# Graph attention on one core: the spread of the queries as two one-pass products of 256 columns

## The reference

```python
q = (x @ Wq + bq).reshape(n, 8, 16); k, v = the same with Wk, Wv
scores = sum(q[targets] * k[sources], -1) * 0.25 + (edge_attr @ We + be)
e = exp(scores - segment_max(scores, targets)[targets])
probs = e / (segment_sum(e, targets) + 1e-10)[targets]
agg = segment_sum(probs[:, :, None] * v[sources], targets)
out = layernorm(x + agg @ Wo + bo)
```

## Time and profile before

| | |
|---|---|
| median of 3 runs | 2608.14 us (2605.48 to 2614.73) |
| the profiled execution | 2609.25 us, span 2607.4 us |
| PE matmul | 1395.8 us busy, 54%; 9699 records, and as many loads of weights |
| DVE | 1341.0 us busy, 51% |
| POOL | 1521.0 us busy, 58% |
| ACT | 420.9 us busy, 16% |
| mean granted clock of TensorE | 0.647 of full speed |
| DMA | 290.29 MB, mean 111 GB/s |

### The profile page before, as it was taken

One profiled execution on the slowest core, in us unless ns is written; L12 is line 12 of the kernel. 1 busy time (PEld: TensorE's weight loads), 2 busy tenths in 40 slices (PEclk: granted clock), 3 DMA queues, 4 the chain that ended last, 5 costly groups with the idle time before them and its releaser, 6 DMA issues.

```text
span 2607.4 us, 30805 instructions
## 1 busy us (share of the span) xinstructions
PE 1395.8 (54%) x9699; PEld 933.4 (36%) x9699; DVE 1341.0 (51%) x3136; ACT 420.9 (16%) x1427; POOL 1521.0 (58%) x1578
## 2 busy tenths in 40 slices
PE   4145555455645464555555555546464545555557
PEld 3033333333433343333334333334343333333334
DVE  4045455554555554545555545555454545555556
ACT  0011111111111111111111111111111111111112
POOL 6735656566566566565556565656566665656540
PEclk7555666666667666666666666666566666566666
DMA  7423333333333333333333333333333333333320
GB/s 271 140 82 97 117 103 103 118 102 124 100 118 106 120 103 121 101 109 113 101 119 105 118 108 117 104 116 106 120 104 123 100 124 95 108 117 106 119 88 7
DMA packets 115466, 290.29 MB, mean 111 GB/s; under 512 B 45765, under 2 KB 53712, under 8 KB 108264
## 3 DMA queue, kind: packets, MB, share of 16 engines
q0 software_dynamic: 75072, 205.10, 26.3%
q1 hardware_dynamic: 37484, 76.52, 8.7%
q10 hardware_dynamic: 2748, 6.69, 0.7%
HBM read 276.52 MB, written 11.67 MB: 111 GB/s over the span
## 4 chain that ended last, share of the span: by engine, by line
another core or an unknown queue 37%; PE 34%; DVE 18%; issue 8%; ACT 2%; DMA 1%; SPq 0%; DVEq 0%; ACTq 0%
PE q_banks L1133 12%; PE ps_a L1170 7%; DVE prod L780 4%; DVE score L791 3%; PE ps_e L1145 2%; PE ps_t L1110 2%; PE ps_s L1191 2%; DVE wv L801 1%; PE ps_t L1116 1%; DVE run_fwd L843 1%; PE ps_a L1212 1%; PE ps_s L1197 1%; PE ps_a L1222 1%; DVE cand L837 1%
## 5 line engine op out<-in xcount | busy, mean ns | idle before, releaser
L507 POOL DMA_INDIRECT kv_buf<-kv_table,src_i x1564 | 1499.1, 959 | 1013.8 <-DVE wv L801 569.0
L1133 PE MATMUL q_banks<-q_blk,hots 64*128 64x128 f32 x3128 | 416.4, 405 | 537.3 <-issue 263.0
L1133 PEld LDWEIGHTS q_banks<-q_blk,hots 64*128 64x128 f32 x3128 | 319.4, 277 | 655.1 <-issue 635.0
L567 ACT ACTIVATE hots<-ps_t 128x512 f32<-128x512 f32 x377 | 225.1, 597 | 1972.9 <-PE ps_t L1116 960.8
L780 DVE TENSOR_TENSOR prod<-q_banks,kv_buf 128x512 f32<-128x512 f32 (+1 forms) x392 | 269.0, 686 | 410.8 <-remote 265.5
L801 DVE TENSOR_TENSOR wv<-kv_buf,ps_w 128x512 f32<-128x512 f32 (+1 forms) x392 | 265.6, 678 | 362.8 <-remote 334.8
L1170 PE MATMUL ps_a<-wv,hots 128*64 128x136 f32 x3128 | 376.5, 379 | 5.6 <-ACT wv L608 4.8
L1212 PE MATMUL ps_a<-sums_sb,carry_from 128*1 128x136 f32 x112 | 34.3, 409 | 542.2 <-DVE sums_sb L911 542.2
L791 DVE TENSOR_REDUCE score<-prod 128x32 f32<-128x512 f32 (+1 forms) x392 | 267.1, 681 | 7.9 <-issue 0.2
L1170 PEld LDWEIGHTS ps_a<-wv,hots 128*64 128x64 f32 x3128 | 239.9, 183 | 68.3 <-issue 51.2
L1212 PEld LDWEIGHTS ps_a<-sums_sb,carry_from 128*1 128x1 f32 x112 | 4.8, 81 | 564.1 <-DVE sums_sb L911 564.1
(11 more groups left out here) (141 smaller groups left out, 1337.5 us busy)
## 6 DMA issues: line engine op xcount, KB each, us to landing
edge_f<-in_edge_blk SPq DMA_DIRECT2D x55, 1024.0 KB
kv_buf<-kv_table,src_i POOLq DMA_INDIRECT x1564
kv_table<-kv_buf ACTq DMA_DIRECT2D x12, 512.0 KB, 4.4
xt_blk<-in_x_t SPq DMA_DIRECT2D x114, 32.0 KB
out<-y_out SPq DMA_DIRECT2D x114, 32.0 KB
kv_buf<-in_x_perm SPq DMA_DIRECT2D x5, 512.0 KB, 7.8
codes<-code_table SPq DMA_DIRECT2D x108, 10.5 KB
code_table<-kv_buf SPq DMA_DIRECT2D x1, 1344.0 KB
```

The lines of the kernel that those rows point to most:

```text
L507: pool.indirect_dma_start(kv_buf[:, b % NBUF, t, :], None, kv_table, bass.IndirectOffsetOnAxis(ap=src_i[:, column:column + 1], axis=0)).th ...
L567: one = act.activation(hots[:, v % 2, :, :].rearrange("p k n -> p (k n)"), ps_t[:, :], ACT.Relu, bias=1.0)
L1133: one = pe.matmul(ps_q[j][:, k * D:(k + 1) * D], hots[own, (v - 1) % 2, 0, k * P:(k + 1) * P], q_blk[own, b % QBUF, :], start=True, stop=True)
```

## The change

`spread_q` no longer makes four matmuls of 64 rows. For each pair of tiles it makes two matmuls of 128 rows and 256 columns, which accumulate in PSUM. The moving operand is `q_part`, in the rounded 32-bit format (float32r): for each half of the window its own 128 columns, with zeros in the other half's rows, once with the rounded queries (part 0) and once with what the rounding left (part 1). So a pair's 128 rows give both tiles at once. `hots` has that format too, and the sums by node read it as float32 through a bitcast.

- Removed: `q_blk`, and per step four matmuls of 64x128 by 64x128 float32.
- Added on PE: per step four matmuls of 128x128 by 128x256 float32r.
- ACT `copy_q`: three copies (64x128, 64x128, 128x128) in place of one, and a wait for `s_qlow` of the block before.
- DVE: `low_q`, two subtractions of 64x128, at the end of slot 6 of every block (three of them ahead of the loop), and one memset of 128x1536 in the setup.
- PSUM: a step's queries stand in one bank, steps alternate between two, and the spread of step q waits for the multiply of step q-2, no longer q-1.

```diff
-        hots = sb("hots", [P, 2, 2, QUAD * W])
+        hots = sb("hots", [P, 2, 2, QUAD * W], F32R)
-        q_blk = sb("q_blk", [P, QBUF, D])
+        q_full = sb("q_full", [P, D])
+        q_part = sb("q_part", [P, QBUF, 2, 2 * D], F32R)
-        q_banks = ps("q_banks", [P, 2, 512])
-        ps_q = [q_banks[:, i, :] for i in range(2)]
+        ps_q = [ps(f"ps_q{i}", [P, 512]) for i in range(2)]
             def copy_q(b):
                 act.wait_ge(s_newq, b + 1)
+                if b >= 1:
+                    act.wait_ge(s_qlow, b)
                 if b >= QBUF:
                     act.wait_ge(s_byedge, FIRST[b - QBUF + 1])
-                act.copy(q_blk[:, b % QBUF, :], new_q).then_inc(s_qcopied, 1)
+                act.copy(q_part[0:W, b % QBUF, 0, 0:D], new_q[0:W, :])
+                act.copy(q_part[W:P, b % QBUF, 0, D:2 * D], new_q[W:P, :])
+                act.copy(q_full[:, :], new_q).then_inc(s_qcopied, 1)
+            dve.memset(q_part[:, :, :, :].rearrange("p b k d -> p (b k d)").bitcast(F32), 0.0)
+            def low_q(b):
+                dve.wait_ge(s_qcopied, b + 1)
+                dve.tensor_tensor(q_part[0:W, b % QBUF, 1, 0:D], q_full[0:W, :], q_part[0:W, b % QBUF, 0, 0:D], ALU.subtract)
+                dve.tensor_tensor(q_part[W:P, b % QBUF, 1, D:2 * D], q_full[W:P, :], q_part[W:P, b % QBUF, 0, D:2 * D],
+                                  ALU.subtract).then_inc(s_qlow, 1)
             def multiply(q):
-                dve.tensor_tensor(prod[:, q % 2, 0:n * D].rearrange("p (k j d) -> p j k d", j=2, d=D),
-                                  q_banks[:, :, 0:n // 2 * D].rearrange("p j (k d) -> p j k d", d=D),
-                                  kv_buf[:, b % NBUF, t0:t1, 0:D].rearrange("p (k j) d -> p j k d", j=2),
-                                  ALU.mult).then_inc(s_product, 1)
+                dve.tensor_tensor(prod[:, q % 2, 0:n * D].rearrange("p (t d) -> p t d", d=D),
+                                  ps_q[q % 2][:, 0:n * D].rearrange("p (t d) -> p t d", d=D),
+                                  kv_buf[:, b % NBUF, t0:t1, 0:D], ALU.mult).then_inc(s_product, 1)
+                    if chain(v, 6) is not None and chain(v, 6) + QBUF < NB:
+                        low_q(chain(v, 6) + QBUF)
             def spread_q(v):
-                pe.wait_ge(s_qcopied, b + 1)
+                pe.wait_ge(s_qlow, b + 1)
                 pe.wait_ge(s_copied, HOTS_TO[v - 1])
-                if q >= 1:
-                    pe.wait_ge(s_product, q)
-                for u in range(t1 - t0):
-                    j, k = u % 2, u // 2
-                    own = slice(j * W, (j + 1) * W)
-                    one = pe.matmul(ps_q[j][:, k * D:(k + 1) * D], hots[own, (v - 1) % 2, 0, k * P:(k + 1) * P],
-                                    q_blk[own, b % QBUF, :], start=True, stop=True)
+                if q >= 2:
+                    pe.wait_ge(s_product, q - 1)
+                for k in range((t1 - t0) // 2):
+                    for part in range(2):
+                        one = pe.matmul(ps_q[q % 2][:, k * 2 * D:(k + 1) * 2 * D], hots[:, (v - 1) % 2, 0, k * P:(k + 1) * P],
+                                        q_part[:, b % QBUF, part, :], start=(part == 0), stop=(part == 1))
             def sum_step(v):
-                    one = pe.matmul(sums(b)[own, :], hots[:, (v - 1) % 2, 1, u * W:(u + 1) * W], wv[:, q % 2, u, :],
+                    one = pe.matmul(sums(b)[own, :], hots.bitcast(F32)[:, (v - 1) % 2, 1, u * W:(u + 1) * W], wv[:, q % 2, u, :],
```

More of the change, by code:

```diff
@@ L283, in graph_attention @@
         s_weighted, s_beside, s_summed = sem("s_weighted"), sem("s_beside"), sem("s_summed")
-        s_newq, s_qcopied = sem("s_newq"), sem("s_qcopied")
+        s_newq, s_qcopied, s_qlow = sem("s_newq"), sem("s_qcopied"), sem("s_qlow")
         s_changes, s_runends = sem("s_changes"), sem("s_runends")
@@ L941, in _ @@
             with dve.If(general == 0):
+                for b in range(min(QBUF, NB)):
+                    low_q(b)
                 for v in SLOTS:
```

## The result

| | before | after |
|---|---|---|
| median of 20 runs of each, on one chip | 2610.67 us (2601.36 to 2624.11) | 2622.47 us (2609.46 to 2629.64) |
| ratio | | 1.0045, interval 1.0029 to 1.0060 |
| the profiled execution | 2609.25 us, span 2607.4 | 2614.39 us, span 2612.6 |
| matmul records of PE | 9699 | 8135 |
| mean granted clock of TensorE | 0.647 | 0.654 |

The account below looks back on a forecast made before the run. It took POOL's gathers, held up by DVE's weighting because PE's results come late while gathers are in flight, as the bound. Gains 8 + 50 + 5 less 3 of costs make 60 us: 2548 us, range 2450 to 2660.

Parts of the forecast that it names:

- What bounds the kernel: Steady block of 44.1 us: POOL waits for DVE's weighting because PE's results come late while gathers are in flight.
- PE, fast stretches: Spread on the chain of slots 1 and 2: match begins after 1.0 us instead of 1.16; 8 us less.
- PE, late stretches: Spread while gathers fly: eight fewer matmuls and loads bring later sums forward, 0.9 us a block; 50 us less.
- Second bank: Slot 6: the spread need not wait for the multiply; nothing alone, its effect counted in the 50 us.
- The start: First steps of the kernel: spread of step 1 about 10 us instead of 20.5; 5 us less, ends 0 and 20.
- Costs: Slot 6: ACT's extra copies and DVE's subtractions, mostly covered; 3 us more in all.
- A: Drains stay, since lateness ignores PE's instruction count or sums still miss the drain; 10 us less, 2598; chance 0.25.
- B: DVE and ACT of slot 6 are the bound, each block pays 0.9 us; 50 us more, 2658; chance 0.15.
- C: Spread's rounded products are not one-pass, 3.4 us per spread; 250 us more, 2860; chance 0.05.
- D: PE stops being late, the waits of 3.0 and 3.8 us go; some 370 us less, 2240; chance 0.07.

Follow-up runs that it names:

- turns_and_crossing: Changed kernel with PE's turn_ends first in slot 1 and DVE's crossing_maxima in slot 2 behind the weighting; 2534.24 us, ratio 0.9677 to the kernel before.
- no_low_part: Changed kernel with one ACT copy of the queries and no DVE subtraction from the fourth block on; 2055.09 us, ratio 0.9998 to the kernel before.
- crossing_later_old: Kernel before with crossing_maxima, DVE's two scans, moved one slot later to slot 2 behind the weighting; 2054.15 us, ratio 0.9989.

## Why the prediction was wrong

**What bounds the kernel.** Right for late chips: POOL starves, and results come late while gathers are in flight. Halving the gathers took 795 us away. But I held it for a property of the kernel; on chips in time the bound is POOL's 35.1 us a block. The changed kernel itself did not run there, but with `crossing_maxima` moved in both, the two forms take 2054.42 and 2054.15 us: the change is worth nothing.

**PE, fast stretches (-8).** The match begins 1.02 us after the first matmul of the spread (1342.93 to 1343.95 in the changed kernel), 1.0 forecast and 1.16 before. But the multiply starts 1.26 us after it. The 1.26 of the earlier trace rows was read where DVE was busy until 0.09 us before; where it stood idle for the result, it was 1.27:

```profile
1313.80 1.23 PE L1133 MATMUL q_banks<-q_blk,hots 64*128 64x128 f32 x8
1315.07 0.69 DVE L780 TENSOR_TENSOR prod<-q_banks,kv_buf 128x512 f32<-128x512 f32 x1 [0.38 <-PE q_banks L1133]
```

What DVE waits for became no shorter, so the 8 us could not come.

**PE, late stretches (-50).** This step failed. Its first half came true: the spread of step 1 fell from 20.51 to 9.28 us, 10 forecast. What failed is the step from there to the block: "I take 0.9 us a block, about one wait of 3.4 in four blocks". I counted drain waits by their number and gave each one price. Their number stayed at two a block, and their price depends on what DVE has queued between the late result and the weighting that POOL waits for. With the new spread DVE gets one slot further before each drain, from slots 5 and 1 to 6 and 2, and so the second drain falls ahead of the scans: 3.6 + 6.3 = 9.9 us in place of 3.0 + 3.8 + 2.0 = 8.8. The prediction said "the next step is late in its place" and never asked which instructions that next place has ahead of its weighting. `turns_and_crossing` is the evidence that this order is what hides the gain: with the scans out of that place the same spread gives 3.2% on one late chip, and the same moves without it, on another, nothing. How much of this is the scans' 3.35 us themselves is not shown, since the two moves also spread the waits over other steps.

One term of that sum was also mis-read. The 2.9 us of lateness at 1324.93 are 4.13 less 1.26, but 1.26 belongs to a granted clock of 0.5; at 1323.15 the clock was 1.00 and the same spread was back after 0.76 us:

```profile
1323.15 0.71 PE L1133 MATMUL q_banks<-q_blk,hots 64*128 64x128 f32 x8
1323.91 0.69 DVE L780 TENSOR_TENSOR prod<-q_banks,kv_buf 128x512 f32<-128x512 f32 x1 [0.33 <-PE q_banks L1133]
```

At 1324.93 the clock was 1.00 too, so the lateness there was 3.4 us. That would have made the forecast gain larger, not smaller.

**Second bank.** Not measured apart.

**The start (-5).** 11.4 us by block 5, inside the ends of 0 and 20.

**Costs (+3).** On a late chip no run measured them apart; in time `no_low_part` put them at 0.9998 of the kernel before, where they lie beside POOL.

**The rivals.** *A* was nearest: POOL's total wait is within 15 us of 569, as it asked (580.1), though in two waits a block instead of three. Its sum of -10 us against +12 measured lacks the same term. *B* had the right direction for a wrong reason: its sign came true, the fold no longer starts at the drain (L922 at 1342.03, while gathers run; its remote waits fell from 327.0 us to 80.4), but because the drain moved on, and the wait of 6.3 us stands in slots 1 and 2, far from slot 6's work. *C* is excluded by four records in 1.19 us. *D*, which I gave 0.07 because the sums and turns keep their instructions, is what chips in time do to every version with all its gathers, about 2055 us, for a reason that has nothing to do with the change. The Trainium skill's rule that transfers can't slow a compute engine (SBUF — State Buffer, section "SBUF: two separate sides") was set against rows 2 to 4. On chips in time the runs agree with it: gathers at the full rate, a spread back after 1.23 us. On late chips halving the gathers took 30.5% off, on chips in time 20.0%. So transfers alone are not the cause; something that is there in some runs and not in others must come to them, and no run shows what. Slower transfers are not it: the packets of the gathers' queue take 26.3% of a span of 2607.4 us before and 34.0% of 2053.1 in `crossing_later_old`, 686 and 698 us for a DMA engine on average. Nor is the clock, 0.647 and 0.669.

**What stays open.** What makes PE's results late, and whether it belongs to the chip; which part of the new spread shortens the lateness (fewer instructions, full-height weights, the format, the second bank); which of the two moves is needed, since each by itself met only chips in time; and what the changed kernel and the one with both moves take there.

## What to carry to other kernels

Where one engine starves in a cycle, don't price its waits by number. For each place at which it can starve, list what the engine that feeds it has queued between the late result and the instruction that frees the buffer: a speed-up elsewhere moves the starving to a new place, and its price with it. A shorter operation and a new order of the work can each be worth nothing and together several per cent, so try the order once more after the change. And run before and after on more than one chip before a wait is called the kernel's own.

## What the runs showed that was not expected

- The same kernel takes 2051 to 2056 us on some chips and 2608 to 2634 on others, with the same busy time on DVE (1331.3 us in `crossing_later_old`, 1341.0 before) and gathers of the same 0.95 us. The difference shows in PE's results, late while gathers run, 20.5 us for a spread of 1.23, and so in POOL's wait for the weighting: 569.0 us before, 0.6 in `crossing_later_old`.
- On a late chip PE's lateness falls with the form of the spread, 20.5 to 9.3 us at nearly the same column time (records of 1.23 and 1.19 us), and 3.5 us for a match in both.
- Rounded products of 128 columns take 316 ns each, of 256 columns 345 ns (granted clocks 0.837 and 0.823).
